# A state-space layer: every fourth product with C goes to GpSimd, from a copy that ScalarE takes out of PSUM

## The reference, cut to what matters

```python
delta = softplus(x @ W_delta + b_delta)
Bm = x @ W_B;  Cm = x @ W_C                  # 16 columns each, one for each state
A = -exp(A_log)                              # (128, 16)
def step(h, inp):                            # over the tokens of a sequence
    x_t, d_t, B_t, C_t = inp
    bar_A = exp(min(d_t[..., None] * A, 10.0))
    bar_B = clip(d_t[..., None] * B_t[:, None, :], -10.0, 10.0)
    h = clip(bar_A * h + bar_B * x_t[..., None], -10000.0, 10000.0)
    y_t = sum(h * C_t[:, None, :], axis=-1) + x_t * D_param
    return (h, y_t)
...
probs = softmax(flat @ W_router);  top 2 of 4 experts
g = silu(xf @ wg) * (xf @ wu);  g = rmsnorm(g, wn);  out = g @ wd
```

## Time and profile before

| | |
|---|---|
| median of 3 runs | 2186.41 us (2182.80 to 2187.88) |
| the profiled execution, its own time | 2167.64 us |
| its span | 2165.7 us |
| busy over the span | PE 1808.7, DVE 1478.9, ACT 1013.0, POOL 731.6 us |
| the state loop, first to last state (L1391 at 104.6 to L1380 at 338.9 us) | 234.2 us |

### The profile page before, as it was taken

How to read it: one execution, slowest core, us unless ns; L and a number is a source line. 1 busy time by engine, 2 the same in 40 slices (tenths; PEclk the granted TensorE clock), 3 DMA queues, 4 the chain that set the end, 5 groups by cost and what they waited for, 6 DMA issues and landing times. The chain is left out here.

```text
span 2165.7 us, 50175 instructions
## 1 busy us (share of the span) xinstructions
PE 1808.7 (84%) x20226; PEld 1196.8 (55%) x20226; DVE 1478.9 (68%) x3575; ACT 1013.0 (47%) x2544; POOL 731.6 (34%) x951
## 2 busy tenths in 40 slices
PE   6678999899978789986677799999999987756596
PEld 4324557556645556643556566777677652234386
DVE  6799995688875665557870477665666479987723
ACT  5535664566644722243412356666666422215243
POOL 2244554455541514214431311000000056533543
PEclk9778999999999999998779999999999998867688
DMA  8000000100026100080034201000000000021187
GB/s 343 1 1 0 1 0 1 75 5 5 5 80 277 42 2 1 1 331 2 2 116 128 65 25 37 13 20 20 21 20 1 1 1 10 19 101 71 32 296 239
DMA packets 57670, 130.63 MB, mean 60 GB/s; under 512 B 13961, under 2 KB 36188, under 8 KB 51808
## 3 DMA queue, kind: packets, MB, share of 16 engines
q1 hardware_dynamic: 54144, 121.32, 15.6%
q0 software_dynamic: 3296, 6.12, 0.8%
HBM read 107.97 MB, written 20.12 MB: 59 GB/s over the span
## 5 line engine op out<-in xcount | busy, mean ns | idle before, releaser
L319 POOL TENSOR_TENSOR arena<-arena 128x4 f32<-128x4 f32 (+2 forms) x97 | 113.9, 1176 | 772.9 <-DVE arena L263 336.4
L3293 ACT ACTIVATE arena<-PS,arena 128x289 f32<-128x289 f32 x256 | 127.4, 509 | 107.7 <-DVE arena L3401 107.7
L1870 POOL TENSOR_TENSOR arena<-arena 128x128 f32<-128x128 f32 x384 | 141.2, 409 | 42.8 <-PE PS L1733 20.0
L3401 DVE TENSOR_REDUCE arena<-PS 128x2 f32<-128x578 f32 x128 | 94.0, 755 | 76.3 <-PE PS L3181 76.3
L3181 PE MATMUL PS<-arena 128*128 128x289 f32 x512 | 135.5, 408 | 2.1 <-DVE arena L3395 0.9
L1806 DVE RECIPROCAL arena<-PS 128x128 f32<-128x128 f32 x96 | 91.5, 954 | 48.2 <-PE PS L1771 48.2
L1256 POOL TENSOR_TENSOR arena<-arena 128x512 f32<-128x512 f32 x64 | 84.0, 1313 | 109.9 <-DVE arena L1401 109.9
L1837 ACT COPY arena<-PS 32x128 f32<-32x128 f32 x384 | 99.5, 259 | 44.7 <-PE PS L1747 39.7
L3181 PEld LDWEIGHTS PS<-arena 128*128 128x128 f32 x512 | 92.2, 190 | 24.1 <-issue 2.2
L366 PE MATMUL PS<-arena 128*128 128x512 f32 x176 | 92.5, 658 | 12.4 <-DVEq L4199 11.7
L1852 ACT ACTIVATE arena<-arena 128x512 f32<-128x512 f32 x96 | 60.6, 631 | 65.7 <-DVE arena L1799 63.4
(11 more groups left out here) (419 smaller groups left out, 4774.2 us busy)
## 6 DMA issues: line engine op xcount, KB each, us to landing
arena<-in_ctx SPq DMA_DIRECT2D x32, 1091.0 KB, 10.2
arena<-in_f_w SPq DMA_DIRECT2D x39, 514.0 KB, 5.0
arena<-in_ctx SPq DMA_DIRECT2D x16, 834.0 KB, 14.7
lists<-arena SPq DMA_DIRECT2D x8, 1040.0 KB, 10.8
arena<-in_f_w SPq DMA_DIRECT2D x32, 256.0 KB, 3.1
arena<-in_ctx SPq DMA_DIRECT2D x16, 512.0 KB, 3.7
arena<-in_mid SPq DMA_DIRECT2D x1, 3796.5 KB, 11.9
arena<-in_late SPq DMA_DIRECT2D x1, 3204.0 KB, 10.3
```

Of the source, the lines that this page charges most:

```text
L319: e.tensor_tensor(x, x, half.broadcast_to(list(x.shape)), ALU.pow).then_inc(*T.done("norm_root", tag))
L1870: k = e.tensor_tensor(dst[:, b], spread(src[:, b, :], [P, HG, S], 1), spread(self.g.C["headmask"], [P, HG, S], 2), ALU.mult)
L3293: e.activation(self.weights(n, k, 0, UL), PS[:, k, 0:UL], ACT.Exp, bias=self.st[:, h, k:k + 1], accum_out=self.st[:, h, 4 + k:5 + k]).then ...
L3401: e.tensor_reduce(self.st[:, n % 2, 2 * k:2 * k + 2], PS[:, 2 * k:2 * k + 2, 0:UL], AXX, ALU.max, negate=True).then_inc(*T.done("k3_least" ...
```

## The change

For the states with j mod 4 = 1 (16 of 64), the C product is no longer DVE's. ScalarE copies the bank CB into one of two new SBUF tiles `cs` (in its step j+2, ahead of all else in that step), and GpSimd multiplies the scanned state by it (in its step j+3, after that step's u times x). PE may reuse CB once the copy is made. In the changed kernel the moved product is L1271, the copy L1204, and later lines have moved down by 4 to 15.

```diff
+        self.cs = [room.take(QW) for _ in range(2)]
...
+    def by_pool(self, j):
+        return j % 4 == 1
...
-                over_partitions(self.CB, j, SN + j % SN, "a0_c", ("a0_read", j))
+                over_partitions(self.CB, j, SN + j % SN, "a0_c", ("a0_c_copied" if self.by_pool(j) else "a0_read", j))
...
         for i in range(self.STEPS):
+            j = i - 2
+            if 0 <= j < self.STATES and self.by_pool(j):
+                for w in T.due(("a0_c", j), ("a0_read", j - 8)):
+                    e.wait_ge(*w)
+                e.copy(self.cs[j // 4 % 2], PS[:, self.CB, :]).then_inc(*T.done("a0_c_copied", j))
             if i % 4 == self.EXPERT % 4:
...
                 e.tensor_tensor(u, u, g.XT[:, self.part(j)], ALU.mult).then_inc(*T.done("a0_u", j))
+            j = i - 3
+            if 0 <= j < self.STATES and self.by_pool(j):
+                h = self.Ur[:, j % self.RING, :]
+                for w in T.due(("a0_c_copied", j), ("a0_scanned", j)):
+                    e.wait_ge(*w)
+                e.tensor_tensor(h, h, self.cs[j // 4 % 2], ALU.mult).then_inc(*T.done("a0_read", j))
...
             j = i - 3
-            if 0 <= j < self.STATES:
+            if 0 <= j < self.STATES and not self.by_pool(j):
```

More of the change, by code:

```diff
@@ L68 @@
         "last_turned": "cols_turned", "sel_turned": "cols_turned", "yturned": "cols_turned", "kc_out": "lin_out", "bc": "lin_out",
-        "z": "lin_out", "z_out": "lin_out", "rows": "rows_out", "ffn_hidden": "lin_out", "products": "lin_out",
+        "z": "lin_out", "z_out": "lin_out", "c_copied": "cols_act", "rows": "rows_out", "ffn_hidden": "lin_out", "products": "lin_out",
         "query_out": "lin_out", "located": "lin_out", "select": "cleared",
```

## The result

The changed kernel takes **2202.1 us** (median of 6 runs, 2195.0 to 2208.4) against 2185.0 us for the kernel before in the same comparison (6 runs, 2179.3 to 2195.2): a ratio of 1.0073, 95% interval 1.0055 to 1.0092, so about 16 us slower. The forecast was 2206.5 us with a range from 2194 to 2219, and 88% for slower.

The account below looks back on a forecast made before the run. Bound: the SBUF access shared by scan, clip and GpSimd products, with PE nearly full beside experts. Terms 3.7 + 2.7 + 12 + 1.7 = 20.1 us on 2186.4 gave 2206.5 us, range 2194 to 2219.

Parts of the forecast that it names:

- quiet steps 4 to 16: Changed steps without expert work: 0.5 us lost in step 4, 1.02 each in steps 8, 12 and 16.
- steps 20 and 21: Last changed step without expert work: two DVE instructions from PSUM hide most of the delay, leaving 0.1 us.
- unit 0: First expert unit, step 23 on: three table loads behind the copy delay silu and PE; 4.8 + 1.0 - 3.1 = 2.7 us.
- steps 26 to 63: Later expert units: PE waits for the silu behind the copy; 10.8 to 14.8 us, taken as 12.
- tail: End of the loop: PE's sum of state 61 waits for GpSimd's moved product, +1.7 us.
- The port: Scan, clip and GpSimd's SBUF products take turns; a quiet changed step becomes 1.02 us longer, not 0.60 shorter.
- a gain: Rival, 5%: waiting GpSimd products give way to scan and clip, so DVE saves up to 9.6 us: 2177 us.
- term for PE's waits in the units: Expert units: silu behind the copy, about 1.7 us in seven units; sum 14.8, less at most 4.0 slack, taken as 12.
- the port alone: Rival, 15%: the silu's delay is covered, leaving 3.7 + 6.4 + 1.7 = 11.8 us: 2198 us.
- The clock: Rival, 12%: PE's rests in the units start half-speed stretches, some 2.5 us each; four give +10: 2216 us.
- The drain: Rival, 4%: each of 11 table-load chains is 1.4 us longer, about 15 us more: 2222 us.
- No difference: Rival, 7%: the lock binds only in part and the saved 0.60 pays the rest: within 4 us of 2186.

Follow-up runs that it names:

- the repeat: The changed kernel run again with no edit, for a second profile: 2193.7 us, loop +20.7 us against the kernel before.
- extra products: Kernel before plus 16 unused GpSimd products of x by x into a spare tile; no copies, DVE keeps all its products: ratio 1.0061 to before.
- memset: Changed kernel with GpSimd's moved product replaced by a memset of a tile, which reads none: one run, loop +2.6 us against before.
- half product: Changed kernel with GpSimd's product cut to 256 of 512 columns, the rest left unmultiplied: one run, loop +7.8 us against before.
- run without copies: Changed kernel without ScalarE's copies; GpSimd multiplies x by x into a spare tile, the 16 C products are left out: ratio 1.0043 to before.
- late copy: Changed kernel with ScalarE's copy of C moved behind the silu and scaling of its step: ratio 1.0070 to before.
- copies alone: Kernel before plus ScalarE's 16 copies; DVE keeps all products and waits for the copy: ratio 1.0054 to before.
- expert part only: Changed kernel with the five states up to 17 given back to DVE, the move holding from state 21 on: ratio 1.0059 to before.

## Why the prediction was right, point by point

| term | forecast, us | measured, us |
|---|---|---|
| quiet steps 4 to 16 | 3.6 | 3.4 to 3.6 |
| steps 20 and 21 | 0.1 | 1.3 |
| unit 0 (steps 24, 25) | 2.7 | 4.5 |
| steps 26 to 63 | 12 | 6.3 (11.0 in the repeat) |
| tail | +1.7 | -1.2 (+0.5 in the repeat) |
| loop | 20.1 | 14.4 (20.7 in the repeat) |

**The port** was right to a few hundredths: scan 1.90, clip 1.42, 1.02 us for each quiet changed step, 0.5 for step 4. Working a step through from the earlier trace rows, with who waits served when the other ends, gave lengths that no view of the kernel before showed. Extra products, memset and half product confirm it from three sides. The rival "a gain" is out by this.

**Steps 20 and 21** went wrong: 1.3 us for 0.1. The moved product starts 0.47 us ahead of the scan, and yet the scan runs first:

```profile
165.97 2.74 POOL L1271 TENSOR_TENSOR arena<-arena 128x512 f32<-128x512 f32 x1
...
166.44 1.21 DVE L1411 TENSOR_TENSOR_SCAN arena<-arena 128x512 f32<-128x512 f32 x1
...
167.57 1.42 DVE L1416 TENSOR_SCALAR arena<-arena 128x512 f32<-128x512 f32 x1
```

I had the product finish before the scan. But this overtaking is only part of the loss: step 20 loses 0.4 us, and step 21 another 0.9, where u times x takes 2.16 us in place of 1.27 although no instruction of DVE beside it reads two SBUF tiles until the scan of 170.11:

```profile
169.07 2.16 POOL L1265 TENSOR_TENSOR arena<-arena 128x512 f32<-128x512 f32 x1 [0.36 <-DVE arena L1416]
...
170.11 2.20 DVE L1411 TENSOR_TENSOR_SCAN arena<-arena 128x512 f32<-128x512 f32 x1
```

The run without copies shows a product on other data overtaken and drawn out to 2.51 us at the same place, so the operands are not the cause of the overtaking; there the next u times x takes 1.27, and the two steps lose 0.2 us. Where the product comes behind DVE's own C product as well (extra products alone) it takes 1.04 us and nothing is lost. Why the first to start isn't served first here, and why the next u times x is long, stays open. Both came again in the repeat and with the late copy.

**Unit 0** was too small by 1.8 us, and by three terms. The table loads cost 2.2 us (late copy: gone) where 4.8 + 1.0 - 3.1 = 2.7 were worked out, so that term was near. Step 24 lost 2.25 us beside it. Of these 0.6 are the port: the scan is held up for 1.0 us more, and 0.3 come back, since DVE has one product less there. The prediction had this 0.65 us for step 24 in its working for the units and left it out of this sum. The other 1.6 are PE at half clock, which was in no term: its broadcast of C begins 2.88 us behind the end of step 23's clip, where it began 1.26 behind. That figure is 2.9 with the late copy and in the run without copies, 2.8 with the copies alone, 2.7 with half the product, but 1.25 with the extra products alone, and 0.4 us ahead of the clip's end with the memset and in the expert part only. It came alike in both executions of the changed kernel. Which clock PE has there I can't derive; that part stays open.

**The step that failed** is the size of the term for PE's waits in the units: 12 us, of a sum of 14.8 less at most 4.0 of slack, where 6.3 were lost (11.0 in the repeat, of which 5 are the clock in unit 4). The waits came as worked out: 17.2 us against 4.0, so 13.2 more, where 14.8 were forecast. What was wrong is what they are worth at the end. PE's time in the stretch adds up so: waits for the silu +13.2; its other idle time 8.9 - 4.0 = 4.9 before and 19.3 - 17.2 = 2.1 now, -2.8; its busy time 123.95 to 119.85, -4.1 (the granted clock of the stretch rose from 0.96 to 0.98, and the records are 531 in place of 537, so part of this may be missing records). Together +6.3, which is the 6.3 of the stretch. I had capped the slack at 4.0, and had looked at idle time only; that PE's busy time could shrink was not considered. Nor is it shown what made it shrink.

That the terms overlap was right. With the late copy the port alone loses 5.0 us from step 25 to 63, the extra products 5.4; the copies with the port free (memset) lose 3.9, the copies alone 9.9 with the clock's 4.8 in them; both at once lose 6.3. The ratios say the same of the whole: extra products 13 us, copies alone 12, both at once 16. So the port, without PE's waits for the silu, already costs nearly all, as in the rival "the port alone" (11.8 us, 15%), and the silu's waits add 1.3 us to the late copy's 5.0 and not 6. But the two shares are so near to each other, in single profiles and within the ratios' intervals, that which of them is the larger is not shown.

That the total came out so near is in part luck. Steps 20 and 21 and unit 0 lost 3 us more than their terms, the tail gave 2.9 back, and the units lost 5.7 less than theirs. By the ratio's interval the change costs 12 to 20 us; 20.1 is at its upper end and 11.8 at its lower, so the total doesn't choose between the forecast and that rival; the late copy does. The forecast's own range of 2200 to 2214 also has a lower end that its terms don't give: with 10.8 us for the units they sum to 2205.

**The clock** rival was right in kind: one fall of 4 to 5 us in unit 4 in the repeat, with the copies alone and with the states j mod 4 = 2, none in the first profile. **The drain**: the Trainium skill, "ScalarE: Activation LUTs", "What ACT_TABLE_LOAD costs", adds 1.38 us behind each load. Here the silu starts 1.30 us after its load begins (201.93 to 203.23), so there is no such gap, and the measured time is not 2222 us. **"No difference"** is out by the interval.

**The tail** had the right mechanism and a missed partner. PE's sum of state 61 does start 1.7 us later than the delay alone would have it (347.94, against 329.46 + 16.8 = 346.26 with 15.5 of delay and the loop's start 1.3 later):

```profile
346.62 1.26 POOL L1271 TENSOR_TENSOR arena<-arena 128x512 f32<-128x512 f32 x1
...
347.94 1.12 PE L1117 MATMUL PS<-arena 128*128 128x512 f32 x2
...
354.55 0.75 DVE L1395 SCALAR_TENSOR_TENSOR arena<-arena,PS 128x512 f32<-128x512 f32 x1 [3.33 <-PE PS L1117]
```

But before, that sum took 2.06 us at half clock, and the work behind it too (granted clock 0.50 from 329.4 to 335.1); now it takes 1.12 at full clock, and 2.8 us come back.

## What to carry to other kernels

Before work is moved from VectorE to GpSimd, add up what the two of them read from SBUF in one period, not their busy times: here u times x, scan and clip filled a 2.75 us period, so a product moved from the side that reads PSUM to the side that reads SBUF cost 1.02 us where it saved 0.60. Here the operation with a PSUM operand was the wrong one to move, since it had cost the port nothing. Place matters second: the copy ahead of three table loads cost 2.2 us, and the products ahead of a small result that another engine waits for cost 9 us more over the loop (16.2 against 7.4). And a wait by PE need not be worth its length: here 13.3 us of them could be removed, and the loop fell by less than 1 us.

## What the runs showed of the hardware that was not expected

- A GpSimd memset of 128x512 (0.53 us) runs inside a scan without touching it; a GpSimd product of the same size takes turns with it.
- GpSimd's product of a tile with itself into a third one holds the port for 0.84 us behind a scan, that of two different tiles in place for 1.07, one of 256 columns for 0.54 less.
- A GpSimd product that had started 0.47 us ahead of a scan was overtaken by it (2.74 us long); in a quiet step u times x, 0.45 us ahead (140.74 and 141.19), was not.
- In step 21 a u times x took 2.16 us in place of 1.27, with only DVE instructions that read PSUM beside it for its first 1.04 us; what held it is open.
- After the same wait of 4.98 us PE's granted clock was back at full 3 us into the work in one execution, and at half for 10 us more in another of the same program: 5 us of difference.
